# Routed token tiles turned into columns by VectorE's 32x32 block turn, from loads that come in squares

## The reference

```python
def ffn(x):                                  # x: 2048 tokens x 512
    y = swiglu(x, sw1, sw2, sw3)             # shared experts, 704 wide
    scores = softmax(x @ gate_w)             # 8 experts
    weights, indices = top_k(scores, 2)
    cw = zeros(N, 8).at[arange(N)[:, None], indices].add(weights)
    for e in range(8):                       # routed experts, 352 wide
        y = y + cw[:, e:e+1] * swiglu(x, rw1[e], rw2[e], rw3[e])
    return y

def swiglu(x, w1, w2, w3):
    return (silu(x @ w1) * (x @ w3)) @ w2

x = x + 0.5 * ffn(layernorm(x))
x = x + attention(layernorm(x))
x = x + 0.5 * ffn(layernorm(x))
```

## Time and profile before

| | us |
|---|---|
| median of 3 runs | 1653.01 |
| lowest and highest of them | 1652.7, 1659.41 |
| the profiled execution | 1639.62 |
| its span, first to last instruction | 1637.8 |
| TensorE busy | 1574.1 |
| GpSimd busy | 895.6 |
| VectorE busy | 868.7 |
| ScalarE busy | 655.9 |

### The profile page before, as it was taken

How to read it: one execution, slowest core, us unless ns; L and a number is a source line. 1 busy time by engine, 2 the same in 40 slices (tenths; PEclk the granted TensorE clock), 3 DMA queues, 4 the chain that set the end, 5 groups by cost and what they waited for, 6 DMA issues and landing times.

```text
span 1637.8 us, 24221 instructions
## 1 busy us (share of the span) xinstructions
PE 1574.1 (96%) x8412; PEld 1147.1 (70%) x8412; DVE 868.7 (53%) x1484; ACT 655.9 (40%) x972; POOL 895.6 (55%) x745
## 2 busy tenths in 40 slices
PE   8999999999998899999999999999999999999996
PEld 6778898999886774444444444336778898998985
DVE  5554322222277686777777777766554422222226
ACT  4422222232233315666666666763431222222321
POOL 4107477405666856788888878510405286433635
PEclk9999999999999898999999999999999999999998
DMA  9306455324272331112112121123105265333337
GB/s 344 130 8 246 168 186 187 132 78 148 97 236 93 84 75 42 33 31 48 29 36 43 31 39 21 23 51 133 58 1 181 99 228 181 132 133 132 133 92 255
DMA packets 89345, 180.16 MB, mean 110 GB/s; under 512 B 30224, under 2 KB 31120, under 8 KB 86928
## 3 DMA queue, kind: packets, MB, share of 16 engines
q1 hardware_dynamic: 75968, 104.41, 21.3%
q0 software_dynamic: 12832, 73.67, 12.6%
q10 hardware_dynamic: 432, 0.54, 0.1%
HBM read 106.48 MB, written 55.97 MB: 99 GB/s over the span
## 4 chain that ended last, share of the span: by engine, by line
PE 68%; DMA 11%; DVE 8%; POOL 4%; issue 3%; SPq 3%; ACT 3%; POOLq 0%; DVEq 0%; ACTq 0%
PE PS L1204 9%; PE PS L1206 9%; PE PS L1205 9%; PE PS L1437 7%; PE PS L1451 6%; PE PS L1418 6%; DMA xn<-x_routed 4%; DMA xs<-x_routed 3%; PE PS L1467 2%; PE PS L1341 2%; PE PS L1346 2%; PE PS L1344 2%; PE PS L1343 2%; PE PS L1345 2%; PE PS L1342 2%
## 5 line engine op out<-in xcount | busy, mean ns | idle before, releaser
L1705 ACT ACTIVATE PT<-PS 128x1024 f32<-128x1024 f32 x256 | 258.2, 1025 | 127.1 <-PE PS L1437 125.3
L2007 DVE TENSOR_REDUCE nmf_later<-PS 128x1 f32<-128x1024 f32 x160 | 194.2, 1219 | 59.2 <-PE PS L1418 58.9
L1451 PE MATMUL PS<-PT,V 128*32 128x512 f32 x1024 | 203.3, 607 | 0.0
L2075 POOL TENSOR_TENSOR W<-raw,W 128x544 fp32r<-128x544 f32 x144 | 190.3, 1356 | 1.5
L1437 PE MATMUL PS<-QS,KS 98*128 98x512 f32 x512 | 179.0, 433 | 4.0 <-DVE nmf_later L2007 3.8
L997 POOL TENSOR_TENSOR added<-PT 128x1024 f32<-128x1024 f32 x56 | 136.0, 2429 | 78.4 <-ACT PT L1705 78.4
L1437 PEld LDWEIGHTS PS<-QS,KS 98*128 98x128 f32 x512 | 85.7, 191 | 129.2 <-issue 51.6
L1418 PE MATMUL PS<-KS,QS 96*128 96x512 f32 x512 | 169.5, 413 | 3.6 <-DVE nmf_first L2007 1.6
L1974 DVE TENSOR_TENSOR thid<-thid,PS 128x352 f32<-128x352 f32 x78 | 40.7, 521 | 245.7 <-ACT thid L1636 245.7
L2063 POOL DMA_DIRECT2D raw<-ffn_w x18 | 10.0, 557 | 248.0 <-POOLq L2061 191.3
L1204 PE MATMUL PS<-xh,W 128*128 128x512 f32 x352 | 140.4, 399 | 4.7 <-DVE xl L1732 2.1
(11 more groups left out here) (206 smaller groups left out, 3845.1 us busy)
## 6 DMA issues: line engine op xcount, KB each, us to landing
raw<-ffn_w POOLq DMA_DIRECT2D x18, 2176.0 KB, 10.4
y_routed<-ytile SPq DMA_DIRECT2D x78, 256.0 KB, 2.1
xn<-x_routed SPq DMA_DIRECT2D x40, 256.0 KB, 2.9
x_routed<-xq SPq DMA_DIRECT2D x1, 9984.0 KB, 29.4
xs<-x_routed SPq DMA_DIRECT2D x38, 256.0 KB, 4.0
QS<-later_hi SPq DMA_DIRECT2D x112, 64.0 KB, 2.0
raw<-ffn_w SPq DMA_DIRECT2D x6, 768.0 KB, 6.6
raw<-ffn_w SPq DMA_DIRECT2D x16, 272.0 KB, 4.3
```

The source lines that it names most:

```text
L1451: e.matmul(PS[i * QUARTER:(i + 1) * QUARTER, ob, :], V[:, b * QT + kt, g, :], PT[:, u % PTBUF, kt % 2 * GRP:(kt % 2 + 1) * GRP], start=rou ...
L1705: e.activation(PT[:, u % PTBUF, :], PS[:, i:i + 2, :].rearrange("p b n -> p (b n)"), ACT.Exp, scale=SCALE).then_inc(p_ready.sem, 1)
L2007: e.tensor_reduce(row_maxima(n)[:, h, t:t + 1], PS[:, i:i + 2, :].rearrange("p b n -> p (b n)"), AX.X, ALU.max, negate=True).then_inc(max_ ...
L2075: low = e.tensor_tensor(W[:, slot, 1, cs], raw[slot][:, cs], W[:, slot, 0, cs], ALU.subtract)
```

## The change

The tile comes from DRAM in four DMAs. DMA q brings columns 128q to 128q + 127 of all 128 tokens to partitions 32q to 32q + 31: token 32a + i goes to partition 32q + i, at columns 128a to 128a + 127. VectorE's `transpose` then turns every 32x32 square of the 128x512 buffer in place of four turns by TensorE and writes the same bank 7. There partition 32q + j holds, at column 128a + 32c + i, element 128q + 32c + j of token 32a + i. The view `xcolumns` reads the bank so that chunk c has its 128 tokens side by side; ScalarE's and VectorE's splits of the tile (`xth`, `xtl`) read it by that view. Chunk c now holds other rows of the inner dimension than before, so the rows of w1 and w3 are put in the same order on the host (`square_rows`).

VectorE turns tile i + 2 at the end of item `tile` i, and tiles 0 and 1 in `tile_start`. TensorE's `turn_tile` is gone. `tile_turned` is now counted by VectorE, and each landing buffer's semaphore rises by 64 for a tile (four DMAs) instead of 16.

```diff
--- before.py
+++ after.py
@@ -22,6 +22,7 @@
 TILES = 2 * TOK // P + E - 1
 ROWS_OUT = TILES * P
 PER_WORD = 8
+SQ = 32
 WORDS = -(-TILES // PER_WORD)
 ROUTE_PIECES = 9
 SPLITS = 8
@@ -651,6 +652,7 @@
     assert at <= wqkv_at + 2 * DC * QKV * 4
 
     PS = ctx.enter_context(nc.psum_tensor("PS", [P, 8, GRP], F32))
+    xcolumns = PS[:, BANK_G, :].rearrange("p (a c i) -> p c a i", a=P // SQ, i=SQ)
     inverse_rows = nc.dram_tensor("inverse_rows", (2, GRP), F32, kind="Internal").ap()
     x_home = nc.dram_tensor("x_home", (TOK, D), F32, kind="Internal").ap()
     x_routed = nc.dram_tensor("x_routed", (ROWS_OUT, D), F32, kind="Internal").ap()
@@ -673,7 +675,7 @@
 
     y_out = signal("y_out", 16)
     scattered = [signal(f"scattered{i}", 32) for i in range(DISPATCH_BUF)]
-    tile_in = [signal(f"tile_in{i}", 16) for i in range(2)]
+    tile_in = [signal(f"tile_in{i}", 16 * P // SQ) for i in range(2)]
     tile_out = [signal(f"tile_out{i}", 16) for i in range(2)]
     gathered = [signal(f"gathered{i}", 32) for i in range(2 * PAIRS)]
     wqkv_in = [signal(f"wqkv_in{c}", 16) for c in range(DC)]
@@ -821,17 +823,20 @@
             s, = key
             for i in range(2):
                 tile_in[i].plan(s, i)
-            for a in (tile_turned, tile_hi, tile_lo):
+            for a in (tile_hi, tile_lo):
                 a.plan(s, 0)
+            for i in range(2):
+                tile_turned.plan(s, i)
         elif kind == "tile":
             s, i = key
             for a in (tile_up, tile_silu, tile_gated, thid_turned, thid_hi, thid_lo):
                 a.plan(s, i)
             if i + 1 < TILES:
-                for a in (tile_turned, tile_hi, tile_lo):
+                for a in (tile_hi, tile_lo):
                     a.plan(s, i + 1)
             if i + 2 < TILES:
                 tile_in[i % 2].plan(s, i + 2)
+                tile_turned.plan(s, i + 2)
             if i:
                 for a in (tile_done, y_ready, tile_out[(i - 1) % 2]):
                     a.plan(s, i - 1)
@@ -1034,6 +1039,14 @@
 
     def sync_program(e):
         sp = Lane(e)
+
+        def tile_load(i):
+
+            for q in range(P // SQ):
+                e.dma_start(xtile[i % 2][q * SQ:(q + 1) * SQ, :].rearrange("i (a n) -> i a n", n=P),
+                            tile_rows(x_routed, i)[:, q * P:(q + 1) * P].rearrange("(a i) n -> i a n", i=SQ)
+                            ).then_inc(tile_in[i % 2].sem, 16)
+
         for kind, *key in work:
             if kind == "start":
                 e.dma_start(identf[:], ident).then_inc(id_in.sem, 16)
@@ -1083,14 +1096,14 @@
                     t = ORDER[-1] * TPG + i
                     sp.wait_ge(scattered[dispatch_place[t] % DISPATCH_BUF], s, t)
                 sp.wait_ge(xn_turned, 2 * s, last_turned)
-                e.dma_start(xtile[0], tile_rows(x_routed, 0)).then_inc(tile_in[0].sem, 16)
+                tile_load(0)
                 sp.wait_ge(a_done, s, last_first)
-                e.dma_start(xtile[1], tile_rows(x_routed, 1)).then_inc(tile_in[1].sem, 16)
+                tile_load(1)
             elif kind in ("tile", "tile_end"):
                 s, i = key if kind == "tile" else (key[0], TILES)
                 if i + 2 < TILES:
                     sp.wait_ge(tile_turned, s, i)
-                    e.dma_start(xtile[i % 2], tile_rows(x_routed, i + 2)).then_inc(tile_in[i % 2].sem, 16)
+                    tile_load(i + 2)
                 if i:
                     sp.wait_ge(y_ready, s, i - 1)
                     e.dma_start(tile_rows(y_routed, i - 1),
@@ -1302,14 +1315,6 @@
             pe.wait_ge(route_done, s)
             e.reg_load(routed["words"], words[0:1, 0:WORDS])
 
-        def turn_tile(s, i):
-            pe.wait_ge(tile_in[i % 2], s, i)
-            until_free(BANK_G)
-            for c in range(DC):
-                turned = e.transpose(PS[:, BANK_G, c * P:(c + 1) * P], xtile[i % 2][:, c * P:(c + 1) * P], identf[:])
-            turned.then_inc(tile_turned.sem, 1)
-            free[BANK_G] = (tile_lo, s, i)
-
         def tile_down(s, i):
             slot, bank = routed["slot"][i], i % 2
             pe.wait_ge(thid_lo, s, i)
@@ -1347,8 +1352,6 @@
             mm.then_inc(tile_up.sem, 1)
             free[BANK_A] = (tile_silu, s, i)
             free[BANK_B] = (tile_gated, s, i)
-            if i + 1 < TILES:
-                turn_tile(s, i + 1)
             if i:
                 tile_down(s, i - 1)
             pe.wait_ge(tile_gated, s, i)
@@ -1510,7 +1513,6 @@
                 s, = key
                 routed["slot"] = {}
                 tile_words(s)
-                turn_tile(s, 0)
             elif kind == "tile":
                 tile(*key)
             elif kind == "tile_end":
@@ -1566,7 +1568,7 @@
             act.wait_ge(tile_turned, s, i)
             if i == 0:
                 act.wait_ge(a_done, s, last_first)
-            e.activation(xth[:], PS[:, BANK_G, :].rearrange("p (c n) -> p c n", c=DC), ACT.Copy).then_inc(tile_hi.sem, 1)
+            e.activation(xth[:].rearrange("p c (a i) -> p c a i", i=SQ), xcolumns, ACT.Copy).then_inc(tile_hi.sem, 1)
 
         def tile_out_of_bank(s, i):
             act.wait_ge(tile_done, s, i)
@@ -1890,10 +1892,16 @@
             e.tensor_tensor(low, hid[where][rows, i, :], hidh[where][rows, i, :],
                             ALU.subtract).then_inc(hid_ready.sem, 1)
 
+        def turn_tile(s, i):
+            dve.wait_ge(tile_in[i % 2], s, i)
+            if i:
+                dve.wait_ge(tile_lo, s, i - 1)
+            e.transpose(PS[:, BANK_G, :], xtile[i % 2]).then_inc(tile_turned.sem, 1)
+
         def tile_columns_lo(s, i):
             dve.wait_ge(tile_hi, s, i)
-            e.tensor_tensor(xtl[:], PS[:, BANK_G, :].rearrange("p (c n) -> p c n", c=DC), xth[:],
-                            ALU.subtract).then_inc(tile_lo.sem, 1)
+            e.tensor_tensor(xtl[:].rearrange("p c (a i) -> p c a i", i=SQ), xcolumns,
+                            xth[:].rearrange("p c (a i) -> p c a i", i=SQ), ALU.subtract).then_inc(tile_lo.sem, 1)
 
         def combine(s, t):
             pair = pairs[s][pair_of_tile[s, t]]
@@ -1967,7 +1975,10 @@
                         e.scalar_tensor_tensor(X[:, t, :], PS[:, j, :], 0.5, X[:, t, :],
                                                ALU.mult, ALU.add).then_inc(shared_added.sem, 1)
             elif kind == "tile_start":
-                tile_columns_lo(*key, 0)
+                s, = key
+                turn_tile(s, 0)
+                tile_columns_lo(s, 0)
+                turn_tile(s, 1)
             elif kind == "tile":
                 s, i = key
                 dve.wait_ge(tile_silu, s, i)
@@ -1976,6 +1987,8 @@
                     tile_columns_lo(s, i + 1)
                 dve.wait_ge(thid_hi, s, i)
                 e.tensor_tensor(htl[:], PS[:, BANK_R, 0:FCH * P], hth[:], ALU.subtract).then_inc(thid_lo.sem, 1)
+                if i + 2 < TILES:
+                    turn_tile(s, i + 2)
             elif kind == "combine":
                 combine(*key)
             elif kind == "wqkv":
@@ -2231,7 +2244,13 @@
 
     a = {k: np.asarray(v) for k, v in inputs.items()}
 
+    def square_rows(w):
+
+        return w.reshape(P // SQ, DC, SQ, -1).transpose(1, 0, 2, 3).reshape(D, -1)
+
     def expert_unit(w1, w3, w2):
+
+        w1, w3 = square_rows(w1), square_rows(w3)
 
         w13 = np.stack([w1.reshape(DC, P, F), w3.reshape(DC, P, F)], 2).transpose(1, 0, 2, 3)
         w2 = np.pad(w2, ((0, FCH * P - F), (0, 0))).reshape(FCH, P, D).transpose(1, 0, 2)
```

## The result

| | before | after |
|---|---|---|
| median, us | 1652.86 | 1638.59 |
| lowest and highest of 4 runs | 1650.82, 1659.41 | 1625.85, 1641.15 |
| the profiled execution | 1639.62 | 1638.36 |

The ratio is 0.9883 with a 95% interval of 0.985 to 0.9916: faster, and clear of the 0.5%. The medians are 14.3 us apart and the ratio stands for 19 us (14 to 25), where the prediction had 22.4.

The account below looks back on a forecast made before the run. TensorE was taken as the bound: -33.4 us for its turns + 11 for late loads = -22.4, so 1617.2 us on the profiled execution and 1630.6 for the median, which lay 13.4 above it; range 1611 to 1655.

Parts of the forecast that it names:

- Four turns from TensorE: Routed tiles of both FFNs: removing TensorE's turns gains 0.44 us in each of 76 tiles, 33.4 us.
- The block turn: VectorE's turn into bank 7 takes 0.69 us, hidden in its 3.10 us of idle time a tile: no cost.
- Reads by squares: ScalarE's and VectorE's reads of bank 7 for xth and xtl take 0 more; 0.25 us of cover remain.
- rival 2: Slower square reads break the 0.25 us cover before the next up projection; up to 1710 us; chance 0.11.
- The deadline 0.3 us nearer: A tile load must land within 9.4 us of issue instead of 9.7, since block turn, xth and xtl follow it.
- The load 0.8 us later in a late place: Beside an expert's load, 24 small rows left per engine delay the tile load 0.8 us; bounds 0 to 1.75.
- rival 3: Small rows travel in groups, so tile loads beside an expert's land earlier; 1609 to 1623 us; chance 0.12.
- The sum of the late places: Ten places where tile loads land late: 0.8 + 0.3 = 1.1 us more each, 11 us.
- rival 1: Late tile loads eat the gain: 10 x 3.35 = 33.5 us, time around 1653 us; chance 0.14.
- The signs that it named: Undisturbed tile 6.28 us, turn 0.55 to 1.2 us behind htl, xth 0.60, xtl 0.69, five late places a stage.
- Landing buffer free at the turn: SyncE's load of tile i + 2 still stands behind the store of tile i - 2; earlier turn gains 0.
- The start of a stage: Turning tile 1 first delays VectorE's four shared-expert additions 0.9 us; their banks are wanted a tile later: 0.

Follow-up runs that it names:

- experiment 2: Changed kernel with SyncE issuing the load of tile i + 4, not i + 2, in item i; 1613.13 against 1656.31 us for the kernel before, 0.9732.
- experiment 3: Kernel before the change, only SyncE's program reordered to issue tile loads early, still one DMA; 1646.83 against 1656.31 us, 0.9941.
- experiment 7: Changed kernel with early tile loads, VectorE's block turn done twice for each tile; 1615.78 against 1657.57 us for the kernel before, 0.9716.
- experiment 8: Changed kernel with early tile loads, xtl computed twice for each tile; 1647.14 against 1657.57 us for the kernel before, 0.9925.
- experiment 5: Changed kernel with four DMAs of 32 whole rows instead of four of squares; 1643.04 against 1657.57 us for the kernel before, 0.9898.
- experiment 4: Changed kernel with one DMA of 128 whole rows instead of four of squares; 1623.62 against 1656.31 us for the kernel before, 0.9789.
- experiment 1: Changed kernel with register values for TensorE's and GpSimd's waits passed once a stage through a maximum; 1636.58 against 1656.31 us for the kernel before, 0.9868.
- experiment 6: Kernel before, TensorE's turns kept, with the changed kernel's four DMAs of squares; 1668.97 against 1657.57 us, 1.0054.

## Why the prediction was right, and what its sum had wrong

- **Four turns from TensorE, 33.4 us.** Right: 34.2 by the period of the stores, 34 to 35 by experiments 2 and 3. That the chain of waits charged them 0.44 us a tile, and not the 0.6 us that an instruction's row shows, was the number to use.
- **The block turn, 0.69 us and hidden.** Right: 0.72 us, and hidden even when doubled (experiment 7).
- **Reads by squares at no cost, cover of 0.25 us.** Right: 0.59 and 0.69 us; the cover is 0.31 to 0.33 us (experiment 8). So rival 2 did not come about, by little.
- **The deadline 0.3 us nearer.** Right: 9.6 became 9.35.
- **The load 0.8 us later in a late place.** The size was nearly right (10.7 to 11.3 us over the shared places, and up to 13.1), the reason is shown in part only. The prediction laid it to 24 small rows left over on each engine when the expert's load ends. That the two loads end together is so, and with squares the tile's ends 0.5 us later behind the expert's than before. But experiment 5 has no small rows and is as late, so small rows are not the whole cause; four DMAs are enough, and how they act stays open. The rule of the Trainium skill ("DMA: Bandwidth & Descriptors", "Queues, rings and completion order"), by which an engine drains a whole packet of descriptors before it turns to the next ring, would by the prediction's working have let the tile's rows pass early; the trace does not agree, since even one DMA of whole rows took 9.5 us beside an expert's load (experiment 4), and rival 3 did not happen.
- **The sum of the late places, 11 us more.** This is the term that was mis-sized: 21.0 us more in the profiles, 14 by the times of experiments 1 to 3. Matched by expert, nine of the ten old places went from 8.3 to 22.8 us, 1.6 us a place where 1.1 were forecast, and the tenth (1.3 us) is gone. Four places are new, with 7.7 us. Of both, 3.7 us are three falls of the clock, which the prediction did not think of: it reckoned a late place as the lateness and nothing else. The new places were foreseen only as rival 1's "more than ten places"; three of them come because the four DMAs take so long to issue that the expert's load falls among them.
- **The signs that it named.** An undisturbed tile, the turn, `xth` and `xtl` came as written. But 13 places, one of them with 13.07 us from issue to turn (1369.14 to 1382.21), are rival 1's signs, and VectorE stood waiting for tile loads outside the ten places, by which the prediction itself said it would fall. So the gain stands as forecast, and the price of the loads lies between the forecast and rival 1, as the time of 1638.59 lies between 1630.6 and 1653. The range held because it allowed up to 2.5 us a place.
- **Landing buffer free at the turn: 0.** Right for the kernel as it was written, since SyncE's own order held the load back. Written so that the order follows the turn, this was worth 23.5 us by the medians of experiments 1 and 2, 29.8 by the late places of the profile. The prediction saw the store in front and stopped there.
- **The start of a stage: 0.** No time is seen lost there; it was not tried by itself.
- **From the profiled execution to the median.** Adding the same 13.4 us was a guess that came out: the prediction gave no reason. The profiles now show one: outside the stages experiment 3 took 14.3 us more than the profile before, and the two stops of TensorE are in that part.

## What to carry to other kernels

Where an engine is the bound, take its own work's price from the period of the loop or the chain, and then ask for each engine behind it how much of its cover the removal takes away. A load that is late beside a bulk transfer was cured here by moving the deadline: look which wait in the issuing engine's program stands in front of the load without need, before working on the load's size. One DMA cut into four was later beside a bulk transfer, and was caught by it more often because its issue takes longer; that cost time only where the deadline was near. And before two profiles are compared, check the stretches that the change does not touch: here they differed by nearly as much as the change was worth.

## What the runs showed of the hardware that was not expected

- SyncE's issue of a DMA took 0.43 us undisturbed and 1.67 us beside an expert's load (at 284.02; 1.96 us at most): 3.1 us for four at 282.58, 1.87 us at 336.17.
- A late tile load beside an expert's 2,176 KB took 9.3 to 12.3 us to the turn in one DMA of 128 rows of 2 KB (experiment 4) and 9.6 to 13.1 us in four DMAs of 512 rows of 512 B; in the median, most of them undisturbed, the four parts land in 2.2 to 2.4 us.
- VectorE's turn of 128x512 float32 from SBUF into a bank of PSUM takes 0.72 us. ScalarE reads a bank in runs of 32 elements in 0.59 us, as it reads it straight.
- The granted clock averaged 0.66 of full speed over 3.5 us after TensorE had been idle for 2.12 us; in experiment 4 it fell behind 0.94 us, and in experiment 6 it once stayed full behind 1.96 us.
